# Mamba and mixture-of-experts on one core: dt from exact bf16 parts, best scores in PSUM, a new order on every engine

## The reference

```python
x = x + mamba(layernorm(x))
x = x + experts(layernorm(x))
# mamba, for one sequence
xi, res = split(x @ W_in)                 # 256 channels each
u = silu(causal_conv4(xi) + conv_b)
dbc = u @ W_x                             # 8 + 16 + 16 columns: delta_r, B, C
delta = softplus(delta_r @ W_dt + b_dt)
h[t] = exp(delta * A) * h[t-1] + delta * B * u    # 256 channels x 16 states
y = (sum over the states of h * C + u * D) * silu(res)
out = y @ W_out
# experts, for one token
scores = x @ gate_w.T                     # 8 scores, the best two are taken
p = softmax(best two)
out = sum over e of cw[e] * (silu(x @ w1[e].T) @ w2[e].T)
```

## Time and profile before

| | |
|---|---|
| median of 3 runs | 1202.45 us (1202.15 to 1203.94) |
| the profiled execution | 1212.32 us |
| its span, first to last instruction | 1210.5 us |
| TensorE busy, mean granted clock | 1095.6 us (91%), 0.965 |
| VectorE, GpSimd, ScalarE busy | 1045.3, 966.2, 889.8 us |
| scans: the first and the last start | 48.7 and 1115.5 us |

### The profile page before, as it was taken

The page is one execution under the profiler, slowest core; times in us unless marked ns, Lnnn a source line. Parts: engine busy times, 40 slices in busy tenths (PEclk is TensorE's granted clock), DMA queues, the critical chain, the costliest instruction groups (busy, mean ns, idle before and its releaser), DMA issues.

```text
span 1210.5 us, 18554 instructions
## 1 busy us (share of the span) xinstructions
PE 1095.6 (91%) x6112; PEld 763.5 (63%) x6112; DVE 1045.3 (86%) x1043; ACT 889.8 (74%) x1349; POOL 966.2 (80%) x896
## 2 busy tenths in 40 slices
PE   4576879999999999999999989999999999887887
PEld 2245466675666676666768666676767666665654
DVE  2499999999999999999989999999999999998211
ACT  4887777876798797778879877889888687863232
POOL 4487887979699897879799796979988888887432
PEclk9788999999999999999999999999999999999999
DMA  4240404030030404022040402121212112020000
GB/s 140 78 158 1 158 1 158 10 140 19 27 141 10 158 10 157 0 91 74 9 157 9 157 10 108 50 88 70 87 71 87 70 51 108 1 87 1 10 9 9
DMA packets 38339, 84.10 MB, mean 69 GB/s; under 512 B 4344, under 2 KB 29184, under 8 KB 29952
## 3 DMA queue, kind: packets, MB, share of 16 engines
q1 hardware_dynamic: 36752, 83.00, 18.8%
q10 hardware_dynamic: 1520, 0.34, 0.1%
HBM read 78.62 MB, written 4.72 MB: 69 GB/s over the span
## 4 chain that ended last, share of the span: by engine, by line
PE 65%; DVE 20%; issue 11%; ACT 3%; POOL 1%; DVEq 0%; POOLq 0%; ACTq 0%
PE work L1030 18%; PE work L1020 14%; DVE h L732 12%; PE y_ps L972 10%; PE work L899 9%; DVE rows L722 3%; PE rows L951 3%; PE work L942 2%; PE work L918 2%; PE work L993 2%; PE work L909 2%; DVE yT L763 1%; PE work L883 1%; DVE weighted L806 1%; DVE top_no L797 1%
## 5 line engine op out<-in xcount | busy, mean ns | idle before, releaser
L414 POOL TENSOR_TENSOR h<-h,c_rows 128x1024 f32<-128x1024 f32 x256 | 601.2, 2367 | 44.4 <-DVE h L732 44.4
L732 DVE TENSOR_TENSOR_SCAN h<-dA,rows 128x1024 f32<-128x1024 f32 x256 | 575.8, 2271 | 0.8 <-ACT dA L620 0.7
L722 DVE TENSOR_TENSOR rows<-du,rows 128x1024 f32<-128x1024 f32 x256 | 306.6, 1215 | 37.4 <-PE rows L951 24.7
L620 ACT ACTIVATE dA<-delta,a_neg 128x510 f32<-128x510 f32 x512 | 324.7, 710 | 1.5 <-issue 0.6
L1020 PE MATMUL work<-x2T,w 128*128 128x512 f32 x512 | 265.7, 617 | 31.0 <-DVE weighted L806 15.0
L972 PEld LDWEIGHTS y_ps<-ident,h 128*128 128x128 f32 x2048 | 242.2, 145 | 49.0 <-issue 41.5
L972 PE MATMUL y_ps<-ident,h 128*128 128x128 f32 x2048 | 268.1, 280 | 0.0
L1030 PEld LDWEIGHTS work<-w,hid 128*128 128x128 f32 x2048 | 247.8, 198 | 29.3 <-ACT hid L650 15.9
L1030 PE MATMUL work<-w,hid 128*128 128x128 f32 x2048 | 254.3, 281 | 4.8 <-DVE yT L763 3.8
L650 ACT ACTIVATE hid<-work 128x512 f32<-128x512 f32 x256 | 151.4, 595 | 134.5 <-PE work L1020 133.1
L454 POOL TENSOR_TENSOR x<-x,weighted 128x512 f32<-128x512 f32 x128 | 163.2, 1275 | 75.3 <-DVE weighted L806 70.2
(11 more groups left out here) (94 smaller groups left out, 950.0 us busy)
## 6 DMA issues: line engine op xcount, KB each, us to landing
c_rows<-c_dram SPq DMA_DIRECT2D x64, 1024.0 KB, 5.0
x_in<-in_x SPq DMA_DIRECT2D x16, 256.0 KB, 2.9
x_again<-in_x SPq DMA_DIRECT2D x16, 256.0 KB, 7.3
out<-x SPq DMA_DIRECT2D x16, 256.0 KB, 2.3
w<-in_w1T SPq DMA_DIRECT2D x1, 1024.0 KB, 6.0
w<-in_w2T SPq DMA_DIRECT2D x1, 1024.0 KB, 8.1
h<-in_conv_w SPq DMA_DIRECT2D x1, 512.0 KB, 4.9
c_dram<-bcd SPq DMA_DIRECT2D x16, 32.0 KB, 5.1
```

Of the source, the lines that this page charges most:

```text
L414: nc.gpsimd.tensor_tensor(at, at, c_rows[:, n, :].unsqueeze(1).broadcast_to([P, H, T]), ALU.mult).then_inc(c_used, 1)
L620: last = nc.scalar.activation(two_seqs(dA[:, n % RING, half, :])[:, :, 1:], two_seqs(delta[:, half, :])[:, :, 1:], ACT.Exp, scale=a_neg[:, ...
L722: nc.vector.tensor_tensor(rows[:, n % 2], du[:, j.odd], rows[:, n % 2, H - 1, :].unsqueeze(1).broadcast_to([P, H, T]), ALU.mult).then_inc( ...
L732: nc.vector.tensor_tensor_scan(h[:, n % RING].rearrange("p h t -> p (h t)"), dA[:, n % RING].rearrange("p h t -> p (h t)"), rows[:, n % 2] ...
```

## The change

It has four parts.

The dt rows now go the way of the B rows. `W_x`'s 8 dt columns are loaded six times, at partitions 16 and 24 of each block of 32, so that `parts` holds all three bf16 parts of dt, twice. `W_dt` is cut into three bf16 parts at the start (10 small VectorE instructions), laid out so that two matmuls over 96 rows give the sum of the products. The C rows move to partition 96.

```diff
-DT_ROW = 3 * SPLIT
-C_ROW = DT_ROW + RANK
+DT_ROWS = (NS, NS + RANK)
+C_ROW = 3 * SPLIT
...
             def delta_rank(j, half, *uses):
...
-                pe.wait_ge(bcd_ready, j.count(1, 1))
+                pe.wait_ge(low_ready, j.count(1, 1))
                 free(*uses)
-                nc.tensor.matmul(work[:, DT[half], :], w_dt[DT_ROW:C_ROW, half * P:(half + 1) * P],
-                                 bcd[DT_ROW:C_ROW, :], start=True, stop=True).then_inc(dt_projected, 1)
+                for step in range(2):
+                    last = nc.tensor.matmul(work[:, DT[half], :], w_dt[:, step, half * P:(half + 1) * P],
+                                            parts[:, j.odd, :], start=(step == 0), stop=(step == 1))
+                last.then_inc(dt_projected, 1)
```

At the start there are more loads, and VectorE's first large instruction waits for the first GpSimd chain:

```diff
-            load(w_bc[:, :, DT_ROW:C_ROW], W_x[:, 0:RANK].rearrange("(h p) n -> p h n", p=P))
+            for part in range(3):
+                for row in DT_ROWS:
+                    load(w_bc[:, :, part * SPLIT + row:part * SPLIT + row + RANK],
+                         W_x[:, 0:RANK].rearrange("(h p) n -> p h n", p=P))
...
+                sp.wait_ge(dt_rows_clear, 1)
+                for part in range(3):
+                    for copy, row in enumerate(DT_ROWS):
+                        at = part * SPLIT + row
+                        sp.dma_start(w_dt_rows[at:at + RANK, copy, :], W_dt).then_inc(dt_rows_loaded, 16)
...
             pre_stats(Round(0))
+            dve.wait_ge(rstd_ready[0], 1)
             dve.wait_ge(taps_loaded, 16 * TAP_LOADS)
```

```diff
             def top_two(j):
...
+                top = work[:, SCORE, TB * E:2 * TB * E].rearrange("p (b e) -> p b e", b=TB)
                 nc.vector.tensor_copy(scores[:, :, :], in_bank).then_inc(scores_ready, 1)
...
-            def top_numbers(j):
-                if not there(j):
-                    return
-                dve.wait_ge(top_at_ready, j.count(1, 1))
-                wait(dve, routing_step, j.count(ROUTING, 0))
-                nc.vector.tensor_copy(top_no[:, :, :], top_at[:, :, 0:2]).then_inc(top_no_ready, 1)
...
             def ratio_exp(j):
                 if not there(j):
                     return
+                exp_tables()
                 act.wait_ge(top_gap, j.count(1, 1))
                 nc.scalar.activation(ratio[:, :], ratio[:, :], ACT.Exp).then_inc(ratio_ready, 1)
+                act.wait_ge(top_at_ready, j.count(1, 1))
+                nc.scalar.activation(top_no[:, :, :], top_at[:, :, 0:2], ACT.Copy).then_inc(top_no_ready, 1)
```

The banks and the lists of all five engines are new:

```diff
-CONV = (0, 1)
-GATE = (0, 1)
+CONV = (1, 0)
+GATE = (1, 1)
...
-HIDDEN = ((0, 1), (0, 1), (1, 0), (1, 1), (1, 0), (0, 1), (1, 0), (1, 0))
-EXPERT = (0, 1, 0, 1, 0, 0, 1, 0)
+HIDDEN = ((0, 1), (0, 1), (1, 0), (0, 0), (1, 0), (0, 1), (0, 0), (1, 0))
+EXPERT = (0, 1, 1, 0, 1, 1, 0, 1)
```

More of the change, by code:

```diff
@@ L307, in round_ @@
             def round_(i):
-                four, five, seven = (i.later(-k) for k in (4, 5, 7))
+                two, three, four, six = (i.later(-k) for k in (2, 3, 4, 6))
+                load_c(four, 3)
                 load_x(i)
[L310 to L316, removed]
+                load_c(three, 0)
+                load_again(four)
+                load_c(three, 1)
+                load_c(three, 2)
+                store_c(two)
+                store_out(six)
             def first_loads():
@@ L331, in _ @@
             first_loads()
[L332 removed]
+            run(sp, round_, 6)
             for odd in range(2):
@@ L652, in round_ @@
             def round_(i):
-                one, two, three, four, five = (i.later(-k) for k in (1, 2, 3, 4, 5))
-                decay(three, 6)
-                decay(three, 7)
-                hidden(five, 0, 0)
-                hidden(five, 0, 1)
-                copy_y(four)
-                hidden(five, 1, 0)
-                hidden(five, 1, 1)
-                exp_tables(three)
-                decay(three, 8)
-                decay(three, 9)
-                decay(three, 10)
-                decay(three, 11)
@@ L697, in round_ @@
-                copy_x2T(four)
-                decay(two, 1)
-                decay(two, 2)
-                decay(two, 3)
-                hidden(five, 6, 0)
-                hidden(five, 6, 1)
-                hidden(five, 7, 0)
-                hidden(five, 7, 1)
-                exp_tables(two)
-                decay(two, 4)
-                decay(two, 5)
-                ratio_exp(four)
+                one, two, three, four = (i.later(-k) for k in (1, 2, 3, 4))
+                decay(two, 14)
@@ new lines, in round_ @@
+                post_norm(three)
+                copy_x2T(three)
+                hidden(four, 6, 1)
+                pre_norm(i)
+                hidden(four, 7, 0)
+                hidden(four, 7, 1)
+                decay(one, 0)
+                copy_xnT(i)
+                decay(one, 1)
+                decay(one, 2)
+                decay(one, 3)
+                decay(one, 4)
+                decay(one, 5)
+                decay(one, 6)
+                ratio_exp(three)
+                conv_silu(i, 0)
@@ new lines, in round_ @@
+                conv_silu(i, 1)
+                decay(one, 7)
+                hidden(three, 0, 0)
+                hidden(three, 0, 1)
+                copy_y(two)
+                hidden(three, 1, 0)
+                hidden(three, 1, 1)
+                decay(one, 8)
+                decay(one, 9)
+                decay(one, 10)
+                hidden(three, 2, 0)
+                skip(i)
+                hidden(three, 2, 1)
+                decay(one, 11)
+                high(i)
+                copy_bcd(i)
@@ L854, in round_ @@
-                inputs(four, 2)
-                inputs(four, 3)
-                top_numbers(six)
-                scan(four, 2)
+                two, three, four, five = (i.later(-k) for k in (2, 3, 4, 5))
+                scan(three, 6)
+                inputs(three, 7)
+                weight_expert(five, 2)
+                inputs(three, 8)
+                scan(three, 7)
+                residual(four)
+                scan(three, 8)
+                next_pre_stats(i)
+                inputs(three, 9)
@@ new lines, in round_ @@
+                inputs(three, 15)
+                top_two(four)
+                inputs(two, 0)
+                scan(three, 15)
+                weight_expert(five, 6)
+                scan(two, 0)
+                inputs(two, 1)
+                scan(two, 1)
+                inputs(two, 2)
+                weight_expert(five, 7)
+                scan(two, 2)
+                inputs(two, 3)
+                inputs(two, 4)
+                scan(two, 3)
+                gating(three)
+                scan(two, 4)
@@ L859, in _ @@
+                inputs(two, 5)
+                weight_expert(four, 0)
+                inputs(two, 6)
+                scan(two, 5)
+                weight_expert(four, 1)
             dve.wait_ge(one_hot_ready, 3)
```

383 lines of the change are left out of this document (186 added, 197 removed).

## The result

The changed kernel takes 1131.9 us, the median of 4 runs (1130.73 to 1132.71); the kernel before took 1202.3, the median of 4 (1193.97 to 1203.94). The ratio is 0.943, with an interval of 0.938 to 0.947.

A forecast was written before the change was run, and what follows sets the result against it. TensorE nearly full (66.2 of 68.75 us a round), VectorE hardly less. Full rounds -29.4, part-filled rounds -3, head -3, tail +3 gave -32: 1180 from the profiled 1212.32, 1171 taken from the median; range 1143 to 1206.

The forecast's parts named there:

- the two parts: Routing (best scores in PSUM, cast on ScalarE) and bf16 dt: 29.4 us less in full rounds, 3 in part-filled ones.
- the dt projection: TensorE: four float32 matmuls a round, 2.10 us, become four bf16 ones, 0.88 us; 1.2 us a round saved.
- VectorE's copies: Two tiny VectorE copies, 3.1 us a round, wait for GpSimd; PSUM source and ScalarE cast save 2.9 us.
- -3 in the head: Up to the first scan: first decay no longer behind a convolution and a table load, -3 us, bounds -6 and +3.
- +3 in the tail: After the last scan's start: hidden halves sharing PSUM banks cost round trips, +3 us, bounds -3 and +6.
- With VectorE 2.9 us lighter I take half of the 2.5 off.: Full rounds: TensorE idles 2.5 us a round, partly waiting for VectorE; half of it, 1.25 us, goes.
- Hidden by 7 us a round: ScalarE: two more table loads and the cast make 57.6 us a round, covered by TensorE's 65.0.
- rival C: Routing too late on GpSimd, so VectorE and then TensorE wait: slower by 23 us, 1225; chance 0.12.
- zero slack worked out for the routing: GpSimd before the first weighting: 15.9 us of work in about 16, so slack of 7 us becomes none.
- B: New order works far better than its parts; TensorE closes up to 65.0 or below, keeps high clock: 1145; chance 0.18.
- A: Only TensorE's own saving counts, the copies' time being hidden behind TensorE: 1187; chance 0.12.
- (D): Savings and new waits cancel; a lighter TensorE that waits more could lose its clock: 1202, no change; chance 0.08.

The follow-up runs named there:

- 1178.4: The kernel before in its old order, with only best scores read from PSUM and the cast of the places on ScalarE: 1178.4 us, ratio 0.983.
- 1153.6: The changed kernel with best scores again in SBUF, copied from SBUF, and the cast of the places on VectorE: 1153.6 us, ratio 0.962.

## Why the prediction was wrong

The direction and the mechanisms of the two parts held; the sum was too small by more than half, because the new order stood in it at nothing. By its own steps:

- **The order. This is the step that failed.** In the sum, -29.4 - 3 - 3 + 3, the full rounds have terms for the dt projection and for VectorE's copies and none for the order and the banks; the order appears only as -3 in the head and +3 in the tail. Measured, it is worth 26 us with both parts in either kernel and 31 without them. Of the 26, 17.8 us fall in the 12 full rounds, 1.5 a round, mostly TensorE's waits for ScalarE at the hidden halves, and 9 to 10 in the tail.
- **The two parts.** Forecast 32 us for them together (29.4 in full rounds and 3 in part-filled ones); measured 39, with the old order kept.
- **"With VectorE 2.9 us lighter I take half of the 2.5 off."** For the parts this came out: TensorE idles (776.6 - 761.8)/12 = 1.2 us a round with both parts in the old order. The order takes it on to (758.8 - 752.5)/12 = 0.5. That the half was met may be luck; it was a guess between none and all.
- **The clock.** The sum left it at 0.98; only the bound had it go back up. In the kernel before it is 0.977 over the full rounds, the mean of 48 equal stretches, and 1.00 in the changed one. By an estimate from these, 0.023 x 68.75 = 1.6 us a round stood there, part of it the profiled execution's own. Most of it comes back with the parts alone (11 falls to 1), which can account for the parts' 39 against 32; that share is argued, not isolated.
- **VectorE's copies.** Forecast 2.9 us a round less, 62.4; measured 62.5 busy, and 166 to 168 ns for each copy of `best`. Right. In the new place the cast proved minor (290 ns) and the copy major.
- **The dt projection.** Forecast 1.2 us a round; 1.5 by the chain in the new order, 1.0 to 2.0 by TensorE's busy time in four pairs. The bf16 matmuls run at 0.22 as forecast. What was not counted is that the float32 ones slow what stands next to them; the row of 0.32 us in the earlier trace rows, taken there for an upper bound of a bf16 matmul, stands right behind one.
- **ScalarE.** Forecast 57.6 us and ten table loads; measured 57.4 and, for the groups at L525, L674 and L558, 60 + 48 + 12 = 120 in 12 rounds. "Hidden by 7 us a round" was wrong as a statement of room: an added 1.3 us came through whole at the one place tried. The two more table loads cost nothing that shows in this order; why was not tested.
- **GpSimd (rival C).** No wait of VectorE for `cw` shows among the waits of the full rounds, and an added 1.2 us cost 0.2 a round. The zero slack worked out for the routing was too pessimistic.
- **Head and tail.** Up to the first full round the forecast has -3 and two part-filled rounds, -5; measured -1.9, and the first scan starts at 47.0 us, where it was 48.7. The tail had +3 for shared banks and -1 for the last round; measured -11.9. Wrong in sign, and the order's.
- **Rivals.** B (1145), that the order works far better than its parts, came nearest, 13 us off. Half of it holds: the order gives 26 us beyond the parts, TensorE closes up and keeps its clock; but the parts give more, 39. The wait of GpSimd for the normalised x, 54.4 us before, is gone from the list of waits, as B had it. A (the copies were hidden anyway) is refuted by 1178.4 and 1153.6. In (D) a lighter TensorE would wait more and lose its clock; it waited less, and the clock rose. B's 0.18 was too little beside the forecast's 0.5, since the forecast had no term at all for what B prices.

## What to carry to other kernels

Price a new order of the lists as a part of its own, and time it alone: here it was, by the medians, the largest of three, and the forecast had it at nothing. When a change takes long waits out of one engine, look at the clock of TensorE behind these waits and count that too. An engine's busy share does not say whether it has room at a given place: here ScalarE at 91% passed on all of 1.3 us and GpSimd at 95% 0.2 of 1.2, and a kernel with 2.5 us less ScalarE work a round was 13 us slower. Ask for each move which instruction stands behind it and who waits for that.

## What was not expected of the hardware

A VectorE copy from SBUF to SBUF of 128x8 numbers waited 5.4 us, over three GpSimd instructions in a row, not over one. The float32 matmul over 8 partitions took 1.05 us where a float32 one over 128 partitions with the same 512 columns takes 0.86, and by the chain the next group took 0.14 us longer. And in the kernel before, TensorE's granted clock fell right behind a pair of these 8-partition matmuls in 8 of 12 rounds, with no wait of 1 us in the 10 us ahead of it.
